# Layer norms that stand alone: squares in one full-width ScalarE step, summed by VectorE, and the turned rows copied by ScalarE

## The chip, the cores and the metric

The kernel runs on one core of a Trainium2 chip. The metric is the device time of one execution in microseconds (us). TensorE multiplies and transposes, VectorE and ScalarE do element-wise work, GpSimd a part of it, and SyncE issues most transfers.

## The reference

Four blocks run one after the other on 4 x 1024 tokens of width 128 in fp32. Each has a mixing part and a feed-forward part, and after each of the eight parts the sum with its input is normalised:

```
def _layernorm(x, axis=-1, eps=1e-05):
    m = jnp.mean(x, axis=axis, keepdims=True)
    v = jnp.var(x, axis=axis, keepdims=True)
    return (x - m) / jnp.sqrt(v + eps)
...
    x = _layernorm(x + _L0_attn_ref(x, ...), axis=-1)
    x = _layernorm(x + _L0_ffn_ref(x, ...), axis=-1)
...
    x = _layernorm(x + _L3_ffn_ref(x, ...), axis=-1)
```

The parts are a gated recurrence, a slot attention with a top-8 choice, a sparse attention on sampled keys, a two-way choice of experts, a linear attention, a top-2 mixture of experts, a state-space scan and a top-p mixture of experts.

## The kernel before

The activations lie transposed in the SBUF tensor `XT`, 128 channels on the partitions and 4096 tokens along the free dimension, in eight chunks of 512 (`NCH`, `ch`). `XK` is the same in token-major form, `ps` is PSUM in eight banks of 512 columns, `SM` holds small values and `TMP` working space. The kernel is one list of parts: stage 1, a fence, norm 1, a fence, stage 2 and so on. A `fence` makes TensorE, VectorE, ScalarE and GpSimd drain and wait for each other. Norms 6 and 7 are woven into other stages. Those after stages 1, 2, 3, 4, 5 and 8 are parts of their own (`LN_ALONE`), written by `layernorm(k)`. Norm 5 is "routed" (`LN_ROUTE`): it also makes router logits.

A norm's plan is a list of steps, and each engine walks through the same list and does its share of each step, in that order. For chunk i:

- `centre`: TensorE multiplies four 128x128 tiles by the centring matrix `cen`, which turns them to token-major form and subtracts the mean, into PSUM bank `pc[i % 4]`.
- `norm`: ScalarE squares the four tiles one after the other, each with an accumulator that gives the sum of squares (`ss`, line 206, and each is followed by an instruction that reads the accumulator), and then takes the root (`sd`, line 205). VectorE takes the reciprocal (`rs`, line 361) and multiplies the chunk into `XK` (line 210).
- `back`: TensorE transposes the chunk back (line 201) into one of three banks `pt`, and VectorE copies it to `XT` (line 209). In the routed norm ScalarE makes this copy (line 208).

The plan runs `centre` two chunks ahead of `norm`, and `back` one chunk behind. Semaphores of kind `Sig` tie the engines: `ln_cen`, `ln_sq`, `ln_sd`, `ln_rs`, `ln_xk`, `ln_tr`, `ln_xv` (rows copied by VectorE) and `ln_xa` (by ScalarE). In norm 2 TensorE also gathers sampled tokens, eight small matmuls after each turn. In norm 3 ScalarE also copies a piece of weights, 128x512, after each of the first six roots. Norm 8 is the last: it has no `back`, and SyncE stores each chunk of `XK` as the output.

Of the kernel before, what the change touches and what calls it, by code (L numbers as in the profile page):

```python
# [8 lines left out]
ALU = mybir.AluOpType  # L9
ACT = mybir.ActivationFunctionType  # L10
AX = mybir.AxisListType.X
# [6 lines left out]
NCH = T // CH  # L18
# [106 lines left out]
def g3(ap, n):  # L125
    return ap.rearrange("p (n k) -> p n k", n=n)
# [6 lines left out]
def ch(ap, i, k=CH):  # L133
    return ap[:, i * k:(i + 1) * k]


def tile(ap, i):
    return ap[:, i * 128:(i + 1) * 128]
# [12 lines left out]
def of(plan, step):  # L151
    return [a for s, a in plan if s == step]


def build(nc, wp, xT_d, sidx_d, cs_d, vecs_d, out_d):
# [3 lines left out]
    sem = Semaphores(lone)  # L159
# [21 lines left out]
    XT, XK, SM = mem["XT"][:, :], mem["XK"][:, :], mem["SM"][:, :]  # L181
# [3 lines left out]
    def w(name):  # L185
        r, o, c = at[name]
        return W[0:r, o:o + c]
# [5 lines left out]
    def mm(out, lhsT, rhs, start=True, stop=True, **k):  # L193
        return nc.tensor.matmul(out, lhsT, rhs, start=start, stop=stop, **k)  # L194
# [8 lines left out]
    def act(out, x, f, bias=0.0, scale=1.0, acc=None):  # L203
        if acc is None:
            return nc.scalar.activation(out, x, f, bias=bias, scale=scale)  # L205
        return nc.scalar.activation(out, x, f, bias=bias, scale=scale, accum_out=acc)  # L206

    acopy = lambda o, a: nc.scalar.copy(o, a)  # L208
    copy = lambda o, a: nc.vector.tensor_copy(o, a)  # L209
# [38 lines left out]
    LN_ROUTE = {5: ("rwT", 3)}  # L248
# [2 lines left out]
    ln_plans = {}  # L251
    for k in LN_ALONE:
        p = ln_plans[k] = [("centre", (k, 0)), ("centre", (k, 1))]
        for i in range(NCH):
            if i + 2 < NCH:
                p.append(("centre", (k, i + 2)))
            p.append(("norm", (k, i)))
            if k == 8:
                continue
            if i > 0:  # L260
                p.append(("back", (k, i - 1)))
            if k in LN_ROUTE and i > 1:
                p.append(("route", (k, i - 2)))
        if k < 8:
            p.append(("back", (k, 7)))
        if k in LN_ROUTE:
            p += [("route", (k, 6)), ("route", (k, 7))]
    ln_all = [x for k in LN_ALONE for x in ln_plans[k]]
    ln_cen = Sig(sem("ln_centred"), of(ln_all, "centre"))
    ln_sq = Sig(sem("ln_squares"), of(ln_all, "norm"))  # L270
    ln_sd = Sig(sem("ln_deviation"), of(ln_all, "norm"))
    ln_rs = Sig(sem("ln_reciprocal"), of(ln_all, "norm"))
    ln_xk = Sig(sem("ln_normed"), of(ln_all, "norm"))
    ln_tr = Sig(sem("ln_turned"), of(ln_all, "back"))
    ln_xv = Sig(sem("ln_rows_by_dve"), [(k, i) for k, i in of(ln_all, "back") if k not in LN_ROUTE])
    ln_xa = Sig(sem("ln_rows_by_act"), [(k, i) for k, i in of(ln_all, "back") if k in LN_ROUTE])
    ln_xh = Sig(sem("ln_high_parts"), [(k, i) for k, i in of(ln_all, "back") if k in LN_ROUTE])
    ln_xl = Sig(sem("ln_low_parts"), [(k, i) for k, i in of(ln_all, "back") if k in LN_ROUTE])
    ln_lg = Sig(sem("ln_logits"), of(ln_all, "route"))
# [11 lines left out]
    def layernorm(k):  # L291
        ar = arena()
        junk = [ar(512) for _ in range(2)]
        ss, rs, sd = SM[:, 0:32], SM[:, 32:64], SM[:, 480:512]
        src, plan = LN_SRC(k), ln_plans[k]
        last, routed = k == 8 or k == LAST, k in LN_ROUTE
        if last:
            plan = [(s, a) for s, a in plan if s in ("centre", "norm")]
        pc, pt = PS[0:4], PS[4:7]
        q4 = lambda ap, i: ap[:, 4 * i:4 * i + 4]  # L300

        def pe(e):
            for step, (_, i) in plan:
                if step == "centre":
                    if i >= 4:
                        e.wait_ge(*ln_xk.at((k, i - 4)))
                    for j in range(4):
                        r = mm(tile(pc[i % 4], j), tile(src, 4 * i + j), w("cen"))
                    r.then_inc(*ln_cen((k, i)))
                elif step == "back":  # L310
                    if i >= 3:
                        e.wait_ge(*(ln_xa if routed else ln_xv).at((k, i - 3)))
                    e.wait_ge(*ln_xk.at((k, i)))
                    for j in range(4):
                        r = turn(tile(pt[i % 3], j), tile(XK, 4 * i + j), w("ident"))
                    r.then_inc(*ln_tr((k, i)))
                    if k == 2:
                        e.wait_ge(*sa_sel.at("samples"))
                        b = i // 2
                        for c in range(4 * (i % 2), 4 * (i % 2) + 4):  # L320
                            r = mm(PS[7][:, b * 35:(b + 1) * 35], tile(XK, b * 8 + c), SO[:, c * 35:(c + 1) * 35], c == 0, c == 7)
                        if i == NCH - 1:
                            r.then_inc(*sa_xs("samples"))
                elif step == "route":
                    name, g = LN_ROUTE[k]
                    e.wait_ge(*ln_xa.at((k, i)))
                    e.wait_ge(s_w[g], 16)
                    for c in range(4 * i, 4 * i + 4):
                        r = mm(PS[7][:, c * 8:c * 8 + 8], tile(XT, c), w(name))
                    r.then_inc(*ln_lg((k, i)))  # L330

        def scalar(e):
            e.wait_ge(s_eps, 1)
            if k == 5:
                first_weights_high(e, 6)
            for step, (_, i) in plan:
                if step == "norm":
                    e.wait_ge(*ln_cen.at((k, i)))
                    for j in range(4):
                        c = 4 * i + j  # L340
                        r = act(tile(junk[i % 2], j), tile(pc[i % 4], j), ACT.Square, scale=128 ** -0.5, acc=ss[:, c:c + 1])
                    r.then_inc(*ln_sq((k, i)))
                    e.wait_ge(*ln_sq.at((k, i)))
                    act(q4(sd, i), q4(ss, i), ACT.Sqrt, bias=eps).then_inc(*ln_sd((k, i)))
                    if k == 3 and i < 6:
                        acopy(ch(top2_w[0], i), top2_src[i]).then_inc(*t2_high(i))
                elif step == "back" and routed:
                    e.wait_ge(*ln_tr.at((k, i)))
                    acopy(ch(XT, i), pt[i % 3]).then_inc(*ln_xa((k, i)))

        def dve(e):
            if k == 2:
                e.wait_ge(s_idx, 16)
                e.wait_ge(s_w[7], 16)
                copy(sif, sidx.bitcast(I32)).then_inc(*sa_num("samples"))
                e.wait_ge(*sa_num.at("samples"))
                tt(g3(SO, 8), sif.unsqueeze(1).to_broadcast([128, 8, 35]), spread(w("tokid"), 35), ALU.is_equal).then_inc(*sa_sel("samples"))
            for step, (_, i) in plan:
                if step == "norm":
                    e.wait_ge(*ln_sd.at((k, i)))  # L360
                    nc.vector.reciprocal(q4(rs, i), q4(sd, i)).then_inc(*ln_rs((k, i)))
                    e.wait_ge(*ln_rs.at((k, i)))
                    tt(g3(ch(XK, i), 4), g3(pc[i % 4], 4), spread(q4(rs, i), 128), ALU.mult).then_inc(*ln_xk((k, i)))
                elif step == "back" and routed:
                    x, h, l = ch(XT, i), ch(xh_all, i), ch(xl_all, i)
                    e.wait_ge(*ln_xa.at((k, i)))
                    copy(h, x).then_inc(*ln_xh((k, i)))
                    e.wait_ge(*ln_xh.at((k, i)))
                    minus(l, x, h).then_inc(*ln_xl((k, i)))
                elif step == "back":  # L370
                    e.wait_ge(*ln_tr.at((k, i)))
                    copy(ch(XT, i), pt[i % 3]).then_inc(*ln_xv((k, i)))

        def sync(e):
            if last:
                for i in range(NCH):
                    e.wait_ge(*ln_xk.at((k, i)))
                    nc.sync.dma_start(out_d.rearrange("b (n p) d -> p (b n) d", p=128)[:, 4 * i:4 * i + 4, :],
                                      g3(ch(XK, i), 4)).then_inc(s_out, 16)
        def pool(e):  # L380
            if k == 3:
                for i in range(6):
                    e.wait_ge(*t2_high.at(i))
                    gtt(ch(top2_w[1], i), top2_src[i], ch(top2_w[0], i).bitcast(F32), ALU.subtract).then_inc(*t2_low(i))
            if k == 5:
                first_weights_low(e, 6)
        return dict(pe=pe, dve=dve, act=scalar, pool=pool, sync=sync)


# [2342 lines left out]
    for k in range(1, LAST + 1):  # L2732
        s = stages[k - 1]()
# [156 lines left out]
```

## Time and profile before

| what | us |
|---|---|
| listed runs: lowest, median, highest of 3 | 2636.87, 2644.38, 2651.82 |
| profiled execution: span from first to last instruction | 2628.1 |
| TensorE busy (matmul) | 2322.3 (88%) |
| VectorE busy | 1851.4 (70%) |
| ScalarE busy | 1430.5 (54%) |
| GpSimd busy | 1004.3 (38%) |

The profiled execution is listed with its span only; its own time is none of the three. The three times count what lies before the first and after the last instruction too. The shares are means over the whole kernel, and say nothing of which engine holds up a given norm: for that the rows in order of time are read. The mean granted TensorE clock is 0.950 of its full speed.

### The profile page before, as it was taken

To read this page: it belongs to the slowest core of one execution; us is meant where nothing else is said; L and a number is where in the kernel's file an instruction comes from. 1 tells how busy PE (TensorE), PEld (TensorE's weight loads), DVE (VectorE), ACT (ScalarE), POOL (GpSimd) and SP (SyncE) were. 2 spreads that over 40 slices of the span, in tenths; PEclk is the share of its full clock that TensorE was granted. 3 is DMA by queue.
4 is the path that set the end of the run, shared out by engine and by line. 5 is a ranking of instruction groups with operands and counts; after the bars stand their busy time and mean duration, and the time that the engine had idled before them with its cause. 6 is when DMAs were issued, how large, how long until landed. Compare 5 with 4: busy or idle time off the path is not lost. (4 is left out here: it accounts for less than half of the span.)

```text
span 2628.1 us, 34742 instructions
## 1 busy us (share of the span) xinstructions
PE 2322.3 (88%) x12026; PEld 1723.2 (66%) x12026; DVE 1851.4 (70%) x3430; ACT 1430.5 (54%) x3023; POOL 1004.3 (38%) x791
## 2 busy tenths in 40 slices
PE   7686778898999999999989998688888886999998
PEld 3464556686899999899867777233333333677776
DVE  5667556676666666666577776488888886877776
ACT  6231232697544444444365554566666653877787
POOL 4000000210322222222125556589898985222222
PEclk8698899999999999999989999899999998999999
DMA  4000000000000000000011122223332330011112
GB/s 185 0 1 0 1 1 1 1 1 17 1 1 1 1 1 1 1 1 1 9 58 54 61 61 61 69 81 87 84 86 80 88 82 27 19 45 47 46 45 61
DMA packets 47551, 96.46 MB, mean 37 GB/s; under 512 B 5120, under 2 KB 9232, under 8 KB 46864
## 3 DMA queue, kind: packets, MB, share of 16 engines
q1 hardware_dynamic: 47344, 94.22, 11.9%
q8 instruction: 96, 1.57, 0.2%
q14 instruction: 79, 0.65, 0.1%
q0 software_dynamic: 32, 0.02, 0.1%
HBM read 91.34 MB, written 2.88 MB: 36 GB/s over the span
## 5 line engine op out<-in xcount | busy, mean ns | idle before, releaser
L194 PE MATMUL ps<-TMPr 128*128 128x512 f32 (+4 forms) x3840 | 956.4, 401 | 86.2 <-DVE TMP L210 26.5
L194 PEld LDWEIGHTS ps<-TMPr 128*128 128x128 f32 (+3 forms) x3840 | 718.2, 190 | 322.6 <-issue 77.6
L214 POOL TENSOR_TENSOR TMP<-TMP 128x512 f32<-128x512 f32 (+2 forms) x496 | 639.3, 1311 | 645.2 <-ACT TMP L205 463.4
L194 PE MATMUL ps<-TMP 128*128 128x65 f32 (+5 forms) x4352 | 514.2, 286 | 9.8 <-DVE TMP L213 7.8
L194 PEld LDWEIGHTS ps<-TMP 128*128 128x128 f32 (+3 forms) x4352 | 472.0, 191 | 62.5 <-issue 32.8
L205 ACT ACTIVATE TMP<-ps,W 128x256 f32<-128x256 f32 (+2 forms) x528 | 283.5, 584 | 303.2 <-DVE TMP L210 184.1
L194 PE MATMUL ps<-TMP,W 128*128 128x512 f32 (+5 forms) x720 | 367.8, 634 | 52.7 <-POOL TMP L214 14.7
L210 DVE TENSOR_TENSOR TMP<-ps,TMP 128x512 f32<-128x512 f32 (+1 forms) x434 | 252.5, 603 | 108.4 <-PE ps L194 48.8
L205 ACT ACTIVATE TMPr<-ps,W 128x512 fp32r<-128x512 f32 x352 | 242.9, 690 | 91.9 <-PE ps L194 72.1
L214 POOL TENSOR_TENSOR XT<-XT,XK 128x512 f32<-128x512 f32 x128 | 175.9, 1374 | 293.1 <-DVE XK L213 274.8
L194 PEld LDWEIGHTS ps<-TMP,W 128*128 128x128 f32 (+3 forms) x720 | 124.4, 191 | 220.4 <-issue 155.3
L213 DVE SCALAR_TENSOR_TENSOR TMPr<-ps,SM,XK 128x512 fp32r<-128x512 f32 x256 | 190.2, 750 | 91.5 <-ACT XK L205 89.3
L205 ACT ACTIVATE ps<-TMP,SM 128x512 f32<-128x512 f32 x256 | 175.0, 692 | 70.2 <-DVE TMP L2625 69.7
L208 ACT COPY TMP<-ps 128x260 f32<-128x260 f32 (+8 forms) x196 | 84.7, 438 | 221.9 <-PE ps L194 169.6
L194 PE MATMUL ps<-Wr 128*128 128x512 f32 (+1 forms) x768 | 190.3, 365 | 9.1 <-DVE Wr L210 9.0
L205 ACT ACTIVATE TMP<-ps 128x512 f32<-128x512 f32 x144 | 86.1, 598 | 139.4 <-PE ps L194 139.2
L2625 DVE TENSOR_TENSOR_SCAN TMP<-ps,SM,TMP 128x512 f32<-128x512 f32 x128 | 156.0, 1266 | 4.2 <-ACT ps L205 4.1
L2625 DVE TENSOR_TENSOR_SCAN TMP<-ps,TMP 128x512 f32<-128x512 f32 x128 | 148.9, 1206 | 12.7 <-ACT ps L205 8.3
L214 POOL TENSOR_TENSOR TMPr<-TMP,TMPr 128x512 fp32r<-128x512 f32 x72 | 93.8, 1304 | 133.8 <-ACT TMPr L208 133.8
L201 PE MATMUL ps<-W,TMP 128*128 128x128 f32 (+2 forms) x720 | 120.1, 282 | 22.3 <-DVE TMP L210 10.5
L205 ACT ACTIVATE XK<-TMPr,SM 128x512 f32<-128x512 f32 x192 | 137.3, 715 | 0.0
L194 PEld LDWEIGHTS ps<-Wr 128*128 128x128 f32 x768 | 120.9, 193 | 19.1 <-issue 9.4
(188 smaller groups left out, 2523.5 us busy)
## 6 DMA issues: line engine op xcount, KB each, us to landing
TMP<-rows SPq DMA_DIRECT2D x168, 256.0 KB, 3.5
TMP<-gates SPq DMA_DIRECT2D x112, 256.0 KB, 3.3
W<-wp SPq DMA_DIRECT2D x1, 4124.0 KB, 13.6
W<-wp SPq DMA_DIRECT2D x1, 3072.0 KB, 26.4
W<-wp SPq DMA_DIRECT2D x1, 2136.5 KB, 19.7
XT<-xT SPq DMA_DIRECT2D x4, 512.0 KB, 7.5
out<-XK SPq DMA_DIRECT2D x8, 256.0 KB, 2.3
W<-wp SPq DMA_DIRECT2D x1, 1993.0 KB, 15.4
```

What stands on the lines that cost most here:

```text
L194: return nc.tensor.matmul(out, lhsT, rhs, start=start, stop=stop, **k)
L201: turn = lambda out, x, ident: nc.tensor.transpose(out, x, ident)
L205: return nc.scalar.activation(out, x, f, bias=bias, scale=scale)
L208: acopy = lambda o, a: nc.scalar.copy(o, a)
L210: tt = lambda o, a, b, op: nc.vector.tensor_tensor(o, a, b, op)
L213: stt = lambda o, a, s, b, op0, op1: nc.vector.scalar_tensor_tensor(out=o, in0=a, scalar=s, in1=b, op0=op0, op1=op1)
L214: gtt = lambda o, a, b, op: nc.gpsimd.tensor_tensor(o, a, b, op)
L2625: nc.vector.tensor_tensor_scan(Hb[q % 4], Ab[q % 3], Ub[q % 6], first, ALU.mult, ALU.add).then_inc(*h_dve((a, x)))
```

## The change

For the norms that are not routed (1, 2, 3, 4 and 8) there is a new step `square`, one chunk ahead of `norm`. In it ScalarE squares the whole chunk in one instruction, 128x512, into `junk[i % 2]` in SBUF, without an accumulator, and VectorE sums each 128 columns of it with one `tensor_reduce` (line 372 of the changed kernel). ScalarE's square waits for the sum two chunks before, which frees `junk`, and the root waits for the sum of its chunk (`ln_sum`). The copy of the turned rows goes from VectorE to ScalarE. The routed norm is as before.

```diff
         p = ln_plans[k] = [("centre", (k, 0)), ("centre", (k, 1))]
+        p += [("square", (k, 0))] * (k not in LN_ROUTE)
         for i in range(NCH):
             if i + 2 < NCH:
                 p.append(("centre", (k, i + 2)))
+            if i + 1 < NCH and k not in LN_ROUTE:
+                p.append(("square", (k, i + 1)))
             p.append(("norm", (k, i)))
...
-    ln_sq = Sig(sem("ln_squares"), of(ln_all, "norm"))
+    ln_sq = Sig(sem("ln_squares"), [a for s, a in ln_all if s == "square" or s == "norm" and a[0] in LN_ROUTE])
+    ln_sum = Sig(sem("ln_sums"), of(ln_all, "square"))
...
-    ln_xv = Sig(sem("ln_rows_by_dve"), [(k, i) for k, i in of(ln_all, "back") if k not in LN_ROUTE])
-    ln_xa = Sig(sem("ln_rows_by_act"), [(k, i) for k, i in of(ln_all, "back") if k in LN_ROUTE])
+    ln_xa = Sig(sem("ln_rows_by_act"), of(ln_all, "back"))
...
-            plan = [(s, a) for s, a in plan if s in ("centre", "norm")]
+            plan = [(s, a) for s, a in plan if s in ("centre", "square", "norm")]
...
-                        e.wait_ge(*(ln_xa if routed else ln_xv).at((k, i - 3)))
+                        e.wait_ge(*ln_xa.at((k, i - 3)))
...
-                if step == "norm":
+                if step == "square":
                     e.wait_ge(*ln_cen.at((k, i)))
-                    for j in range(4):
-                        c = 4 * i + j
-                        r = act(tile(junk[i % 2], j), tile(pc[i % 4], j), ACT.Square, scale=128 ** -0.5, acc=ss[:, c:c + 1])
-                    r.then_inc(*ln_sq((k, i)))
-                    e.wait_ge(*ln_sq.at((k, i)))
+                    if i >= 2:
+                        e.wait_ge(*ln_sum.at((k, i - 2)))
+                    act(junk[i % 2], pc[i % 4], ACT.Square, scale=128 ** -0.5).then_inc(*ln_sq((k, i)))
+                elif step == "norm":
+                    if routed:
+                        e.wait_ge(*ln_cen.at((k, i)))
+                        for j in range(4):
+                            c = 4 * i + j
+                            r = act(tile(junk[i % 2], j), tile(pc[i % 4], j), ACT.Square, scale=128 ** -0.5, acc=ss[:, c:c + 1])
+                        r.then_inc(*ln_sq((k, i)))
+                        e.wait_ge(*ln_sq.at((k, i)))
+                    else:
+                        e.wait_ge(*ln_sum.at((k, i)))
                     act(q4(sd, i), q4(ss, i), ACT.Sqrt, bias=eps).then_inc(*ln_sd((k, i)))
...
-                elif step == "back" and routed:
+                elif step == "back":
                     e.wait_ge(*ln_tr.at((k, i)))
                     acopy(ch(XT, i), pt[i % 3]).then_inc(*ln_xa((k, i)))
...
-                if step == "norm":
+                if step == "square":
+                    e.wait_ge(*ln_sq.at((k, i)))
+                    nc.vector.tensor_reduce(q4(ss, i), g3(junk[i % 2], 4), AX, ALU.add).then_inc(*ln_sum((k, i)))
+                elif step == "norm":
                     e.wait_ge(*ln_sd.at((k, i)))
...
-                elif step == "back":
-                    e.wait_ge(*ln_tr.at((k, i)))
-                    copy(ch(XT, i), pt[i % 3]).then_inc(*ln_xv((k, i)))
```

What stands in ScalarE's row at the beginning of norm 1, before the change (`ln_centred` is `ln_cen`, `ln_squares` is `ln_sq`; the `SM<-SM` step is the root):

```order
L206 ACTIVATE TMP,SM<-ps 128x128 [waits ln_centred,s_eps,s_fence]
L206 ACTIVATE TMP,SM<-ps 128x128 x3
L205 ACT_TABLE_LOAD
L205 ACTIVATE SM<-SM 128x4 [waits ln_squares]
L206 ACTIVATE TMP,SM<-ps 128x128 [waits ln_centred]
L206 ACTIVATE TMP,SM<-ps 128x128 x3
L205 ACTIVATE SM<-SM 128x4 [waits ln_squares]
```

and with it (`ln_sums` is `ln_sum`, `ln_turned` is `ln_tr`):

```order
L205 ACTIVATE TMP<-ps 128x512 [waits ln_centred,s_eps,s_fence]
L205 ACTIVATE TMP<-ps 128x512 [waits ln_centred]
L205 ACT_TABLE_LOAD
L205 ACTIVATE SM<-SM 128x4 [waits ln_sums]
L205 ACTIVATE TMP<-ps 128x512 [waits ln_centred]
L205 ACTIVATE SM<-SM 128x4 [waits ln_sums]
L208 COPY XT<-ps 128x512 [waits ln_turned]
L205 ACTIVATE TMP<-ps 128x512 [waits ln_centred]
```

The squares of two chunks now stand ahead of the table load and the first root, and each copy of turned rows stands ahead of the square of the chunk three later.

VectorE's row at the same place, before the change (`ln_deviation` is `ln_sd`, `ln_reciprocal` is `ln_rs`):

```order
L361 RECIPROCAL SM<-SM 128x4 [waits ln_deviation,s_fence]
L210 TENSOR_TENSOR XK<-ps,SM 128x512 [waits ln_reciprocal]
L361 RECIPROCAL SM<-SM 128x4 [waits ln_deviation]
L210 TENSOR_TENSOR XK<-ps,SM 128x512 [waits ln_reciprocal]
L209 COPY XT<-ps 128x512 [waits ln_turned]
```

and with it:

```order
L372 TENSOR_REDUCE SM<-TMP 128x4 [waits ln_squares,s_fence]
L372 TENSOR_REDUCE SM<-TMP 128x4 [waits ln_squares]
L375 RECIPROCAL SM<-SM 128x4 [waits ln_deviation]
L210 TENSOR_TENSOR XK<-ps,SM 128x512 [waits ln_reciprocal]
L372 TENSOR_REDUCE SM<-TMP 128x4 [waits ln_squares]
L375 RECIPROCAL SM<-SM 128x4 [waits ln_deviation]
L210 TENSOR_TENSOR XK<-ps,SM 128x512 [waits ln_reciprocal]
```

The copies are gone from it, and a sum stands ahead of each reciprocal, that of the chunk after the reciprocal's own; two sums stand ahead of the first. TensorE's row is the same in both kernels.

## Rows read from the trace of the kernel before

**Rows 1.** The page: length of the profiled execution.

```profile
span 2628.1 us, 34742 instructions
```

**Rows 2.** Timeline of norm 4: start, length, engine, line, operation, [idle before].

```profile
633.89 0.28 ACT L206 ACTIVATE TMP<-ps 128x128 f32<-128x128 f32 x1 [4.03 <-PE ps L194]
...
637.58 0.68 DVE L209 COPY XT<-ps 128x512 f32<-128x512 f32 x1
...
637.79 0.30 ACT L205 ACTIVATE SM<-SM 128x4 f32<-128x4 f32 x1
637.82 0.60 PE L201 MATMUL ps<-W,XK 128*128 128x128 f32 x4
...
638.18 0.17 DVE L361 RECIPROCAL SM<-SM 128x4 f32<-128x4 f32 x1
...
638.38 0.69 DVE L210 TENSOR_TENSOR XK<-ps,SM 128x512 f32<-128x512 f32 x1
...
638.99 0.68 DVE L209 COPY XT<-ps 128x512 f32<-128x512 f32 x1
...
639.15 0.30 ACT L205 ACTIVATE SM<-SM 128x4 f32<-128x4 f32 x1
...
645.42 0.69 DVE L210 TENSOR_TENSOR XK<-ps,SM 128x512 f32<-128x512 f32 x1
...
646.26 1.04 PE L201 MATMUL ps<-W,XK 128*128 128x128 f32 x4 [0.78 <-DVE XK L210]
647.34 0.69 DVE L209 COPY XT<-ps 128x512 f32<-128x512 f32 x1 [0.63 <-PE ps L201]
```

**Rows 3.** Costs by shape: ScalarE and VectorE groups, mean ns of one.

```profile
L205 ACT ACTIVATE TMP<-ps,W 128x512 f32<-128x512 f32 x144 | 95.5, 688 | 115.2 <-PE ps L194 114.9
...
L205 ACT ACTIVATE TMP<-ps 128x512 f32<-128x512 f32 x144 | 86.1, 598 | 139.4 <-PE ps L194 139.2
...
L1196 DVE TENSOR_REDUCE SM<-ps 112x1 f32<-112x1024 f32 x20 | 24.5, 1225 | 20.0 <-PE ps L194 20.0
...
L713 DVE TENSOR_REDUCE TMP<-TMP 128x64 f32<-128x512 f32 x4 | 4.1, 1024 | 0.1
...
L685 DVE TENSOR_REDUCE TMP<-TMP 128x4 f32<-128x256 f32 x8 | 3.3, 412 | 6.9 <-POOL TMP L214 6.9
```

**Rows 4.** Timeline of norm 1: first squares, table load, first reciprocal, last copy.

```profile
53.84 0.28 ACT L206 ACTIVATE TMP<-ps 128x128 f32<-128x128 f32 x1 [7.26 <-PE ps L194]
...
55.00 1.28 ACT L205 ACT_TABLE_LOAD   x1
...
56.70 0.18 DVE L361 RECIPROCAL SM<-SM 128x4 f32<-128x4 f32 x1 [6.60 <-ACT SM L205]
...
68.15 0.69 DVE L209 COPY XT<-ps 128x512 f32<-128x512 f32 x1 [0.21 <-PE ps L201]
```

**Rows 5.** One stretch of norm 1: length, PE busy, weight loads, DVE, ACT, POOL, clock.

```profile
53.80:55.70 1.90, 1.90 (x11) 1.90 (x11) 0.00 (x0) 1.84 (x9) 0.00 (x0) 0.50 0.00 0
```

**Rows 6.** Timeline of norm 2: turns of chunks 4 and 5, last copy.

```profile
161.12 0.28 ACT L206 ACTIVATE TMP<-ps 128x128 f32<-128x128 f32 x1 [8.58 <-PE ps L194]
...
170.31 0.60 PE L201 MATMUL ps<-W,XK 128*128 128x128 f32 x4
...
172.54 0.60 PE L201 MATMUL ps<-W,XK 128*128 128x128 f32 x4
...
177.02 0.69 DVE L209 COPY XT<-ps 128x512 f32<-128x512 f32 x1 [0.34 <-PE ps L201]
```

**Rows 7.** Timeline of norm 3: first square, ScalarE's extra cast, last copy.

```profile
470.45 0.28 ACT L206 ACTIVATE TMP<-ps 128x128 f32<-128x128 f32 x1 [3.32 <-PE ps L194]
...
473.11 0.60 ACT L208 CAST TMPr<-W 128x512 fp32r<-128x512 f32 x1
473.30 0.18 DVE L361 RECIPROCAL SM<-SM 128x4 f32<-128x4 f32 x1 [4.21 <-ACT SM L205]
...
473.62 0.27 ACT L206 ACTIVATE TMP<-ps 128x128 f32<-128x128 f32 x1
...
488.08 0.69 DVE L209 COPY XT<-ps 128x512 f32<-128x512 f32 x1 [0.67 <-PE ps L201]
```

**Rows 8.** Timeline of norm 8: first square, first and last reciprocal.

```profile
2612.16 0.28 ACT L206 ACTIVATE TMP<-ps 128x128 f32<-128x128 f32 x1 [7.14 <-PE ps L194]
...
2615.01 0.18 DVE L361 RECIPROCAL SM<-SM 128x4 f32<-128x4 f32 x1 [5.57 <-ACT SM L205]
...
2624.46 0.18 DVE L361 RECIPROCAL SM<-SM 128x4 f32<-128x4 f32 x1 [0.46 <-ACT SM L205]
```


## The prediction

> **What bounds the kernel now.** Times are in us. I first looked for how much of the kernel the change can touch at all, then read the touched stretches row by row. The profiled execution spans 2628.1 [rows 1]; the listed runs have a median of 2644.4, 16.3 more, and that offset is kept in the sum. The change works only in five stretches, the norms alone after stages 1, 2, 3, 4 and 8. From first square to the end of the last step they last 15.0 [rows 4], 16.6 [rows 6], 18.3 [rows 7], 14.1 [rows 2] and 13.2 (the last reciprocal starts 12.3 after the first square, and the last multiply ends 0.9 after that, as at 638.18 to 638.38 + 0.69) [rows 2, 8]. Together that is 77.3, 2.9% of the span. Each is closed by fences, so nothing outside can overlap with it: what such a stretch loses or gains is lost or gained in full.
>
> Inside norm 4 the reader is to see VectorE without a gap: reciprocal at 638.18, multiply 0.20 later, copy of the turned rows 0.61 later, and a copy occupies it for 0.60 before the next reciprocal (637.58 to 638.18) [rows 2]. That is 1.41 a chunk. ScalarE repeats every 1.36 (637.79 to 639.15) [rows 2], hardly less. The two are balanced. Norm 1 runs the same program. Norm 8 has no turning, so it goes at ScalarE's pace: seven steps in 9.45, 1.35 each [rows 8]. Norm 2 goes at TensorE's pace, 2.23 a chunk (170.31 to 172.54) [rows 6], because the sample gathers lie between its turns. Norm 3 is ScalarE's, since it also makes weight parts there.
>
> **Prices.** The full-width Square has no row before. The same shape from PSUM without a bias tile takes 0.60, with one 0.69 [rows 3]; I take 0.60 and keep 0.69 as upper end. Its time until the next ScalarE step is 0.51, from the 512-wide cast that starts at 473.11 and is followed at 473.62 [rows 7]; the new ScalarE copy is priced the same way, 0.51 until the next and 0.59 until done. The sum over 512 elements into 4 has no row either. A contiguous reduction of 256 takes 0.41 and one of 1024 takes 1.225, which gives 0.68 for 512 on the line between them; a strided reduction of 512 takes 1.02 [rows 3]. Ours is contiguous, so I take 0.68 (0.60 until the next step), with 0.41 and 1.02 as ends. So on VectorE the added sum costs what the removed copy did, 0.60, and its work stays at 0.60 + 0.20 + 0.61 = 1.41. ScalarE's falls from 1.36 to 0.51 + 0.20 + 0.51 = 1.22.
>
> The interpolated 0.68 equals the 0.68 of the copy it replaces [rows 2, 3]. The Trainium skill (VectorE: DVE Perf Modes, Rules for kernel authors) calls `tensor_reduce` the slowest VectorE operation and advises restructuring, which speaks against adding 40 of them. Its perf-mode tier table gives a PSUM-source fp32 copy no fast mode, so by the page the exchange is even in norms with a copy and a pure loss in norm 8. The rows agree as far as they reach, and the sum would be the same by either.
>
> **Where the change adds a wait.** Equal work does not mean equal pace, since the order now closes a loop over two chunks. ScalarE's in-order list is: square i+1, root i, copy i-1, square i+2. The copy waits for the turn of i-1, and square i+2 is queued behind it although its data has long been there. Following it round: copy 0.51, square 0.60, hop to VectorE 0.10 (norm 1's load starts at 55.00 for 1.28, the root behind it takes 0.30, the reciprocal starts at 56.70 [rows 4]), sum i+2 0.60, reciprocal i+1 0.20, multiply 0.69, hop to TensorE 0.15 (645.42 + 0.69 to 646.26), turn 0.60 (637.82), hop 0.04 (646.26 + 1.04 to 647.34) [rows 2]. The total is 3.49 for two chunks, so 1.75 a chunk instead of 1.41. Chunks come in pairs: one step of 1.41, the next of 2.08. Before, VectorE's copy was last in its own list and nothing upstream was queued behind it on ScalarE.
>
> **Norm 4.** The head first. Before, the first reciprocal came 1.6 after the first square: in norm 1 the four squares with their reads end 1.16 after 53.84, where the load starts, and root and hop are 0.40 [rows 4]. Now square 0 and the wait of sum 0 are followed on VectorE by sum 1, whose square starts 0.9 after the first (a chunk's centring at the full clock is half of norm 1's 1.9, below): 0.9 + 0.60 + 0.10 + 0.60 = 2.2. Then 1.41 to reciprocal 1, two loops of 3.49 to reciprocal 5, 2.08 to reciprocal 6, 0.8 to reciprocal 7 (no sum is left ahead of it), and a tail of 0.20 + 0.69 + 0.15 + 1.04 + 0.04 + 0.59 = 2.7 with the slow last turn seen at 646.26 [rows 2]. Sum 16.2 against 14.1: **+2.0**.
>
> **Norm 1.** Same steps, but the centring runs at granted clock 0.50, the lower of TensorE's two levels (1.2 of 2.4 GHz): 11 matmuls in 1.90 [rows 5], and with two overlapping the edges a chunk of eight takes about 1.9. Square 1 therefore starts 1.9 after square 0, and the table load, which stood behind square 0 (55.00), now stands behind square 1: 55.7 + 0.6, load 1.3, root and hop 0.4, reciprocal at 58.0 instead of 56.70. From there 1.41 + 6.98 + 2.08 + 0.8 and a tail of 2.3 with a quick turn are 13.5, against 12.1 from 56.70 to the end of the last copy [rows 4]. **+2.7**.
>
> **Norm 2.** TensorE stays the bound, so the loop hides beneath 2.23 a chunk [rows 6]. What shows is the head's 0.6 and, once no centring is left and TensorE does a chunk in 1.3 (the last copy starts 0.64 after the last turn, so the three turns after 172.54 come in 3.84), one loop wait of 0.9 near the end. **+1.5**.
>
> **Norm 3.** Here ScalarE is the bound: before 1.36 + 0.51 for the cast = 1.87 a chunk, after 0.51 x 3 + 0.20 = 1.73, about the loop's 1.75. The head is 0.35 longer (square 1 before the load), six steps gain 0.13 each and the last one, where the cast is gone, 0.6. **-1.0**.
>
> **Norm 8.** Head 0.35 longer, then VectorE's 1.41 against 1.35; but the last sum comes ahead of reciprocal 6, so the last step is only 0.8. That is 0.8 + 6 x 1.41 = 9.3 against 9.45 [rows 8]. **+0.2**. Its output transfers start with the multiplies and move by the same.
>
> Sum: 2.0 + 2.7 + 1.5 - 1.0 + 0.2 = +5.4, so 2633.5 of span and, with the offset, 2644.4 + 5.4 = **2649.8**, 0.2% more. The other edits (fewer instructions to fetch, the lost accumulator reads) cost nothing: ScalarE is never the bound after them except in norm 3, where they are counted.
>
> **Rivals.**
> - The loop does not show, because the copy is ready earlier than I reckon or ScalarE runs on: then VectorE's 1.41 rules. Norms 1, 4 and 2 keep only their heads, +1.3, +0.6 and +0.6, the others as above: +1.7, 2646.1. For it: ScalarE has 0.2 to spare a chunk. Against it: the order, which nothing relaxes. Chance 0.16.
> - The sum costs what the strided one does, 1.02. VectorE needs 1.75 a chunk even without the loop, the loop 3.83; norm 8 is hit in full. That adds 0.34 to every second chunk of norms 1 to 4, some 12, and to seven of norm 8: +6.4, 2656.2. With the squares and copies at 0.69 too, 2659. At 0.41 instead it takes off 2.4. Chance 0.12 for dear, 0.06 for cheap.
> - Slower by far: the clock. TensorE gets more pauses at 1.75 a chunk, and may be granted the lower level. Centring and turn then take 1.9 + 1.04 = 2.9 [rows 2, 5], so norms 1 and 4 lose 1.2 on seven chunks each, and norm 2, if it is caught, up to 2.2 on eight: 34 over my sum, 2684. It decides from 7.8 more than I reckon, that is, norm 2 caught for four chunks. For it: the last turns of norm 4 already take 1.04 instead of 0.60 [rows 2]. Against it: TensorE pauses in norm 3 much longer per chunk (1.87 pace), and norm 2 leaves it no pauses. Chance 0.03.
> - A gain that can be measured would have to be 13 of the 77.3, a sixth of all five norms. No price above leads there unless the sum were nearly free. Chance 0.02.
>
> **How the numbers follow.** A measurement of this kernel tells about 0.5% from no change; that is 13.2. My forecast has 0.61. It, the hidden loop, and the cheap and the dear sum all lie within 0.5%; only the clock lies beyond. Runs of the same kernel spread over 15, so a true +5 can be read a little beyond: I move 0.05 from same to slower and 0.02 to faster. Same 0.88, slower 0.08, faster 0.04. The cost bounds give 2646 to 2659; the runs' spread, 7.5 either side for one and about half for a median, widens this to 2638 to 2662.
>
> **What would show it.** Squares of 128x512 at 0.60, eight a norm, without accumulator reads; reductions at 0.68 on VectorE. Reciprocals in norm 4 in pairs, 1.41 and about 2.08 apart, and squares that wait for TensorE only because a copy stands ahead. Table load of norm 1 at about 56.3. Norm 3 shorter by one. Wrong: even steps of 1.41 (the loop does not bind), a reduction of 1.0, a granted clock of 0.5 in the middle of norms 1, 2 or 4, or any difference outside the five stretches.

## The result, and the profile after

| | us |
|---|---|
| kernel before, median of 20 runs (lowest, highest) | 2644.43 (2636.81, 2653.74) |
| changed kernel, median of 20 runs | 2654.88 (2642.42, 2670.25) |
| ratio, 95% interval | 1.0035 (1.0019 to 1.0052) |

The change costs about 0.35%, and the interval of the ratio lies above 1. The forecast was 2649.8.

The page of the changed kernel gives this span, 13.7 longer than that of [rows 1]:

```profile
span 2641.8 us, 34502 instructions
```

First norm 4 of the changed kernel in order of time, to be laid beside [rows 2]. Columns as there.

```profile
638.55 3.84 PE L194 MATMUL ps<-W,XT 128*128 128x128 f32 x32 [0.89 <-DVEq L230]
...
642.68 0.67 DVE L372 TENSOR_REDUCE SM<-TMP 128x4 f32<-128x512 f32 x1
...
643.27 0.17 DVE L375 RECIPROCAL SM<-SM 128x4 f32<-128x4 f32 x1
...
643.51 0.58 ACT L208 COPY XT<-ps 128x512 f32<-128x512 f32 x1 [1.20 <-PE ps L201]
644.00 0.60 ACT L205 ACTIVATE TMP<-ps 128x512 f32<-128x512 f32 x1
...
644.48 0.30 ACT L205 ACTIVATE SM<-SM 128x4 f32<-128x4 f32 x1
...
644.63 0.69 DVE L372 TENSOR_REDUCE SM<-TMP 128x4 f32<-128x512 f32 x1 [0.47 <-ACT TMP L205]
...
645.24 0.17 DVE L375 RECIPROCAL SM<-SM 128x4 f32<-128x4 f32 x1
...
645.44 0.69 DVE L210 TENSOR_TENSOR XK<-ps,SM 128x512 f32<-128x512 f32 x1
...
646.18 0.42 PEld L201 LDWEIGHTS ps<-W,XK 128*128 128x128 f32 x4 [0.60 <-DVE XK L210]
646.18 0.66 PE L201 MATMUL ps<-W,XK 128*128 128x128 f32 x4 [0.41 <-DVE XK L210]
...
646.64 0.17 DVE L375 RECIPROCAL SM<-SM 128x4 f32<-128x4 f32 x1
...
646.88 0.58 ACT L208 COPY XT<-ps 128x512 f32<-128x512 f32 x1 [0.70 <-PE ps L201]
```

The reader is to see two things. The square at 644.00 starts 0.49 after the copy at 643.51, and that copy had waited 1.20 for its turn. The square's own data had been there since 642.39 at the latest, when the centring of the first four chunks ended (638.55 + 3.84). And the reciprocal at 645.24 comes 1.97 after the one at 643.27, the next at 646.64 only 1.40 later. The reciprocals of the whole norm are 1.40, 1.97, 1.40, 1.96, 1.46, 1.97 and 0.81 apart, where before it was 1.29 once and then 1.40 to 1.42.

Who waited for whom in norm 4 (us in total, times, longest):

```profile
ACT XT L208 <- PE ps L201: 4.9, 7, 1.5
...
PE ps L201 <- DVE XK L210: 3.5, 5, 1.3
```

ScalarE's copy waits for TensorE's turn seven times in the norm's eight chunks, and everything behind it on ScalarE waits with it. That wait did not exist before, when VectorE copied.

The prices, from the groups by shape (busy us, mean ns of one), first ScalarE's, then VectorE's:

```profile
L205 ACT ACTIVATE TMP<-ps 128x512 f32<-128x512 f32 x184 | 109.9, 598 | 174.6 <-PE ps L194 174.3
...
L208 ACT COPY XT<-ps 128x512 f32<-128x512 f32 x56 | 32.6, 583 | 29.7 <-PE ps L201 29.4
```

```profile
L372 DVE TENSOR_REDUCE SM<-TMP 128x4 f32<-128x512 f32 x40 | 27.3, 683 | 23.0 <-ACT TMP L205 22.6
```

The square has joined the group of 598 ns (184 instead of 144), the copy takes 583 ns, and the sum 683 ns.

The head of norm 1 in order of time, beside [rows 4]:

```profile
54.06 0.60 ACT L205 ACTIVATE TMP<-ps 128x512 f32<-128x512 f32 x1 [7.26 <-PE ps L194]
...
55.68 0.60 ACT L205 ACTIVATE TMP<-ps 128x512 f32<-128x512 f32 x1 [1.03 <-PE ps L194]
56.30 1.28 ACT L205 ACT_TABLE_LOAD   x1
...
57.92 0.18 DVE L375 RECIPROCAL SM<-SM 128x4 f32<-128x4 f32 x1 [0.92 <-ACT SM L205]
```

The second square waits until 55.68 for a centring at the lower clock, the table load stands behind it at 56.30 instead of 55.00, and the first reciprocal follows at 57.92, 3.86 after the first square instead of 2.86.

Measured in this way, from first square to the end of the last copy or multiply, the five norms compare as follows.

| norm | before | forecast | changed kernel |
|---|---|---|---|
| 1 | 15.0 | +2.7 | 17.6 (+2.6) |
| 2 | 16.6 | +1.5 | 17.9 (+1.3) |
| 3 | 18.3 | -1.0 | 17.6 (-0.7) |
| 4 | 14.1 | +2.0 | 15.8 (+1.6) |
| 8 | 13.2 | +0.2 | 13.2 (0.0) |
| together | 77.3 | +5.4 | 82.1 (+4.8) |

So 4.8 of the 13.7 lie in the norms. The rest lies where the change touches nothing, which the prediction had named as a sign of being wrong. The largest piece is stage 5: 665.2 from norm 4 to norm 5 before, 670.3 now, and 1.5 in norm 5 itself. Two windows that begin at the same matmul, near the end of stage 5, show it, the first of the kernel before, the second of the changed kernel (from:to, length, then busy time and instructions of TensorE, weight loads, VectorE, ScalarE and GpSimd, granted clock, transfers):

```profile
1288.59:1302.59 14.00, 13.44 (x118) 12.72 (x117) 5.95 (x15) 2.30 (x5) 0.00 (x0) 1.00 0.00 1
```

```profile
1296.00:1310.00 14.00, 13.44 (x76) 12.19 (x76) 4.55 (x9) 1.92 (x4) 0.00 (x0) 0.63 0.00 1
```

Before, TensorE had the full clock (2.4 GHz) in the whole window; in this execution of the changed kernel it had 0.63 on average, so part of it at the lower level of 1.2 GHz, and 14 us hold 76 matmuls instead of 118.

### The profile page after: what moved, and what is told of

It is laid out like the page before. It is cut to its first block and busy times, and to the rows that moved or that the text cites. A ratio compares the mean times of both kernels' runs of the same rounds, so it can differ in the third digit from the quotient of the medians.

```text
span 2641.8 us, 34502 instructions
## 1 busy us (share of the span) xinstructions
PE 2332.6 (88%) x12026; PEld 1734.7 (66%) x12026; DVE 1857.3 (70%) x3438; ACT 1424.3 (54%) x2775; POOL 1004.4 (38%) x791
## 3 DMA queue, kind: packets, MB, share of 16 engines
q1 hardware_dynamic: 47344, 94.22, 11.9%
## 5 line engine op out<-in xcount | busy, mean ns | idle before, releaser
L205 ACT ACTIVATE TMP<-ps 128x512 f32<-128x512 f32 x184 | 109.9, 598 | 174.6 <-PE ps L194 174.3
## 6 DMA issues: line engine op xcount, KB each, us to landing
W<-wp SPq DMA_DIRECT2D x1, 1993.0 KB, 15.3
```

## The experiments

Each ran in rounds with the kernel before on the same chip. The table has all of them; "clock" is the mean over a kernel's runs of the granted TensorE clock, and "norms" the sum of the five norms in its profile. The first row takes together the 88 runs of the kernel before whose clock is listed; the 20 beside the first measurement have none.

| kernel | median, us | before in the same job | ratio (95%) | clock | norms, us |
|---|---|---|---|---|---|
| before | 2643.4 (88 runs) | | | 0.9439 | 77.3 |
| changed | 2654.88 | 2644.43 | 1.0035 (1.0019 to 1.0052) | 0.9407 | 82.1 |
| changed, again | 2650.84 | 2643.36 | 1.0026 (1.0006 to 1.0045) | 0.9422 | 82.6 |
| pure delay of 4.9 | 2651.85 | 2642.61 | 1.0027 (1.0006 to 1.0049) | 0.9417 | 76.8 + 4.9 |
| the same, TensorE busy | 2651.92 | 2643.36 | 1.0035 (1.0013 to 1.0056) | 0.9438 | 78.0 + 4.9 |
| loop opened | 2642.98 | 2642.61 | 1.0001 (0.9977 to 1.0025) | 0.9445 | 75.6 |
| squares only | 2661.79 | 2642.61 | 1.0064 (1.0044 to 1.0084) | 0.9401 | 88.6 |
| copies only | 2663.49 | 2642.61 | 1.0074 (1.0048 to 1.0099) | 0.9387 | 88.5 |
| changed, TensorE busy | 2652.54 | 2643.36 | 1.0026 (1.0002 to 1.0050) | 0.9447 | 81.9 |
| mixed | 2635.43 | 2643.36 | 0.9988 (0.9962 to 1.0015) | 0.9439 | 71.8 |
| mixed, again | 2633.12 | 2644.71 | 0.9975 (0.9953 to 0.9997) | 0.9453 | 72.5 |
| loop opened, early load | 2645.49 | 2644.71 | 1.0010 (0.9988 to 1.0033) | 0.9423 | 74.0 |

**The loop opened.** One list is reordered:

```diff
-        p += [("square", (k, 0))] * (k not in LN_ROUTE)
+        p += [("square", (k, 0)), ("square", (k, 1))] * (k not in LN_ROUTE)
...
-            if i + 1 < NCH and k not in LN_ROUTE:
-                p.append(("square", (k, i + 1)))
             p.append(("norm", (k, i)))
+            if i + 2 < NCH and k not in LN_ROUTE:
+                p.append(("square", (k, i + 2)))
```

> The changed kernel with the square of chunk i+2 put behind the root of chunk i and ahead of the copy of chunk i-1, on ScalarE and in VectorE's list. Loop theory: the copy no longer stands ahead of the square, the ring over two chunks falls to about 2.6 us, and VectorE's own 1.41 us rules: even steps of 1.41 in norms 1 and 4 instead of 1.40 and 1.96 in turn. Norm 1 16.1, norm 2 17.2, norm 3 17.1, norm 4 14.7, norm 8 13.2 us, 3 us less than the changed kernel together. Price theory (the uneven steps come from the costs of sum and square, not from the order): steps and norms as in the changed kernel.

Norm 4 of it in order of time:

```profile
643.66 0.17 DVE L375 RECIPROCAL SM<-SM 128x4 f32<-128x4 f32 x1
...
643.90 0.58 ACT L208 COPY XT<-ps 128x512 f32<-128x512 f32 x1 [0.49 <-PE ps L201]
644.38 0.30 ACT L205 ACTIVATE SM<-SM 128x4 f32<-128x4 f32 x1
...
644.79 0.60 ACT L205 ACTIVATE TMP<-ps 128x512 f32<-128x512 f32 x1
...
645.06 0.17 DVE L375 RECIPROCAL SM<-SM 128x4 f32<-128x4 f32 x1
```

Behind the copy there now stands the root, for which 0.3 suffices, and the reciprocals come at 643.66 and 645.06, 1.40 apart, as they do in the whole norm but for its last step (1.12). The same instructions with the same prices, in another order, so the uneven steps came from the order. The norms last 15.7, 17.0, 15.8, 13.9 and 13.2, together 75.6 instead of 82.1, and the kernel is level with before. Norm 3 gained more than expected (15.8 instead of 17.1); 0.8 of it is its head, which had the full clock here and the lower one in the changed kernel's profile. The last turns of norms 1 and 4 were on the full clock here too, 0.4 quicker each. Without these three about 4.8 of the 6.5 are left for the order.

**One part alone.** First the squares and sums, with VectorE's copy kept:

```diff
-                elif step == "back":
+                elif step == "back" and routed:
                     e.wait_ge(*ln_tr.at((k, i)))
                     acopy(ch(XT, i), pt[i % 3]).then_inc(*ln_xa((k, i)))
...
+                elif step == "back":
+                    e.wait_ge(*ln_tr.at((k, i)))
+                    copy(ch(XT, i), pt[i % 3]).then_inc(*ln_xv((k, i)))
```

> One part of the change alone: full-width squares summed by VectorE, but VectorE keeps the copy of the turned rows. VectorE then needs 0.60 + 0.20 + 0.61 + 0.60 = 2.0 us a chunk and is the bound in norms 1, 3 and 4: norm 1 20.4, norm 2 18, norm 3 19.5, norm 4 18.3, norm 8 13.2 us, about 12 us over the kernel before in the norms together, ratio about 1.005. If the sum were hidden or much cheaper than its 0.60, the steps would stay below 2.0.

```profile
662.40 0.17 DVE L376 RECIPROCAL SM<-SM 128x4 f32<-128x4 f32 x1
...
662.60 0.69 DVE L210 TENSOR_TENSOR XK<-ps,SM 128x512 f32<-128x512 f32 x1
...
663.21 0.68 DVE L209 COPY XT<-ps 128x512 f32<-128x512 f32 x1
...
663.81 0.68 DVE L373 TENSOR_REDUCE SM<-TMP 128x4 f32<-128x512 f32 x1
...
664.40 0.17 DVE L376 RECIPROCAL SM<-SM 128x4 f32<-128x4 f32 x1
```

That is norm 4, VectorE alone: reciprocal, multiply, copy, sum, reciprocal without a gap, 2.00 for the round. The norms last 19.5, 18.4, 19.8, 17.7 and 13.2, 11.3 over before.

Then the copies alone, with four squares and their accumulators as before:

```diff
-                elif step == "back" and routed:
+                elif step == "back":
                     e.wait_ge(*ln_tr.at((k, i)))
                     acopy(ch(XT, i), pt[i % 3]).then_inc(*ln_xa((k, i)))
...
-                elif step == "back":
-                    e.wait_ge(*ln_tr.at((k, i)))
-                    copy(ch(XT, i), pt[i % 3]).then_inc(*ln_xv((k, i)))
```

> The other part alone: four squares with accumulators as before, and ScalarE copies the turned rows. ScalarE then needs 1.36 + 0.50 = 1.86 us a chunk, in norm 3 2.37: norm 1 17.6, norm 2 17.5, norm 3 21.3, norm 4 16.7, norm 8 13.2 us, about 9 us over the kernel before in the norms together, ratio about 1.0035. If the copy fitted into ScalarE's waits, the steps would stay near 1.41.

```profile
655.74 0.30 ACT L205 ACTIVATE SM<-SM 128x4 f32<-128x4 f32 x1
655.94 0.57 ACT L208 COPY XT<-ps 128x512 f32<-128x512 f32 x1
656.07 0.18 DVE L360 RECIPROCAL SM<-SM 128x4 f32<-128x4 f32 x1 [0.95 <-ACT SM L205]
...
656.41 0.28 ACT L206 ACTIVATE TMP<-ps 128x128 f32<-128x128 f32 x1
...
657.59 0.30 ACT L205 ACTIVATE SM<-SM 128x4 f32<-128x4 f32 x1
```

ScalarE's roots of norm 4 are 1.85 apart (655.74 and 657.59), and it has no gap. The norms last 18.7, 18.2, 21.1, 17.2 and 13.2, 11.2 over before; the first copy costs one long step (2.55 in norm 1, 2.36 in norm 4) that I had left out. Each part alone makes one engine the bound. Together they balance, and then the order decides.

**Where the rest comes from.** The kernel before with idle additions at the ends of three norms:

```diff
+            if k in (1, 2, 4):
+                e.wait_ge(*ln_xk.at((k, 7)))
+                for q in range(4 if k == 1 else 2):
+                    tt(idle[q], ch(XK, q), ch(XK, q), ALU.add)
```

> The kernel before, with four, two and two idle VectorE additions at the ends of norms 1, 2 and 4, 0.61 us each: 4.9 us of pure delay, as much as the changed kernel loses in its five norms (4.8 us in its profile), and nothing else changed. Theory A (the rest of the changed kernel's loss comes from TensorE's clock, whose steps fall elsewhere on the same work once the work is shifted): the time rises by clearly more than the delay, by about 10 us, and the profile shows dips of the granted clock at other places than before. Theory B (the rest has to do with how the changed norms use the engines): the time rises by the delay alone, 4.9 us, ratio 1.0019.

Its median rose by 9.2, near theory A, but the interval of the ratio (1.0006 to 1.0049) holds the pure 1.0019 too. Alone it decides nothing. The changed kernel once more:

> The changed kernel once more. Its twenty runs had a mean granted clock of 0.9407, the thirty of before 0.9438, and at equal clock it was 4.1 us longer by a line through all runs (2.2 us for each 0.001 of clock); its median was 10.4 us longer. If the lower clock belongs to the change: again about 0.941 and about 9 us. If it was chance: a clock near 0.944 and a median about 5 us over before. In the profile the five norms again last 4.8 us longer together in either case.

The median is 7.5 over before, the clock 0.9422: between the two cases. Its profile shows that the surplus wanders. Stage 5, which was 5 longer in the first profile, has its old 665.0 again. Instead it is stage 2 (from the end of norm 1 to norm 2's first square) that takes 102.5 instead of 92.3. The windows of that stage, the kernel before first, then this run:

```profile
68.84:161.12 92.28, 62.29 (x275) 44.07 (x276) 52.92 (x190) 21.85 (x42) 5.74 (x8) 0.72 0.00 0
```

```profile
70.08:172.53 102.45, 73.09 (x274) 48.22 (x275) 52.91 (x189) 22.07 (x43) 5.74 (x8) 0.62 0.00 0
```

The work is the same, and the clock 0.62 instead of 0.72. The end of the stage had the lower level throughout, and still had it at the head of norm 2, which begins at 172.53 and lasts 0.8 longer than in the first profile:

```profile
144.00:175.00 31.00, 26.99 (x73) 15.31 (x72) 10.09 (x17) 6.19 (x17) 0.00 (x0) 0.50 0.00 0
```

The delay was then run with TensorE kept at work in it:

```diff
+            if k in (1, 2, 4):
+                for q in range(12 if k == 1 else 6):
+                    mm(tile(pc[0], q % 4), tile(XK, q % 4), w("cen"))
```

> The kernel with the pure delay of 4.9 us at the ends of norms 1, 2 and 4 (it had a mean clock of 0.9417 and 9 us), with TensorE now given filler matmuls during the delay: 12, 6 and 6, of 0.22 us each, into a PSUM bank that is free by then. Pause theory (a norm during which TensorE stands still more often leaves the lower clock to what comes next): the mean clock returns to before's 0.944, the time is 4 to 5 us over before. Chance theory: the clock has nothing to do with such pauses; it lies anywhere between 0.941 and 0.945.

The timeline of its TensorE at the end of norm 1 shows the fillers, 24 records in 2.84 behind the last turn, and that the next stage starts 0.54 after them:

```profile
68.33 0.63 PE L201 MATMUL ps<-W,XK 128*128 128x128 f32 x4 [0.78 <-DVE XK L210]
68.80 2.84 PE L194 MATMUL ps<-W,XK 128*128 128x128 f32 x24
72.18 0.38 PE L194 MATMUL ps<-W 64*128 64x1 f32 x2 [0.54 <-DVEq L230]
```

The mean clock did return to 0.9438. The median did not follow: 8.6 over before, nearly as without the fillers (9.2), though the interval (1.0013 to 1.0056) also holds the 1.0019 of the delay alone. The profiles show where the clock was gained and where it was lost. Two windows of the delay without fillers, then two of the delay with them, behind norm 1 and at the end of stage 2:

```profile
70.00:76.00 6.00, 3.79 (x8) 1.69 (x9) 2.85 (x11) 0.92 (x1) 0.00 (x0) 0.50 0.00 0
144.50:164.20 19.70, 15.69 (x61) 9.26 (x60) 9.21 (x15) 4.71 (x14) 0.00 (x0) 0.83 0.00 0
```

```profile
70.00:76.00 6.00, 4.92 (x25) 2.60 (x23) 3.17 (x12) 1.79 (x2) 0.00 (x0) 1.00 0.00 0
144.50:172.60 28.10, 24.10 (x58) 12.41 (x57) 9.20 (x15) 4.81 (x14) 0.00 (x0) 0.50 0.00 1
```

With the fillers the full clock held behind norm 1, and the end of stage 2 was at the lower level instead. The stage took 103.0, and 94.9 without them. Whether the fillers caused the second is open; the repeated changed kernel, without fillers, had it too. The changed kernel with fillers:

```diff
+                    if k in (1, 3, 4):
+                        for q in range(1 if i < 7 else 4):
+                            mm(tile(PS[7], q), tile(XK, 4 * i + q), w("cen"))
```

> The changed kernel, with one filler matmul of 0.22 us on TensorE after each turn of norms 1, 3 and 4, and four after the last turn, into the PSUM bank that is unused there. TensorE then works 1.55 of 1.68 us a chunk instead of 1.33. Pause theory: the mean clock rises from 0.9407 to about 0.944, and the time falls from about 10 over before to about 5. Chance theory: the clock stays as the repeated changed kernel shows it in the same job. The norms' own lengths stay within 0.5 us of the changed kernel's.

The same again: clock 0.9447, the highest but one, and a median 9.2 over before, with the norms at 81.9; this interval (1.0002 to 1.0050) too holds the 5 us that the pause theory expected. So the medians speak against the pause theory, and do not exclude it. A line through all runs (below) says more: at equal clock the two kernels with fillers are 8.4 and 10.1 over before, and the same kernels without them 3.4, and 4.6 and 3.8. A mean granted clock over the whole span is no measure of what the clock costs when filler work raises it.

**A version from both.** The form of before in norms 1, 2, 4 and 8, the loop-free new form in norm 3, and one early root:

```diff
+            if k in (1, 3, 8):
+                act(sd[:, 31:32], eps, ACT.Sqrt)
```

> The kernel before in norms 1, 2, 4 and 8, the loop-free order of the new form (root of chunk i, square i+2, copy i-1) in norm 3 alone, and in norms 1, 3 and 8 a one-column root at the very start, so that the table load of 1.28 us lies in the wait for the first centring. Expected: norm 1 14.2, norm 2 16.6, norm 3 14.9, norm 4 14.1, norm 8 11.9 us, together 5.5 us less than before, ratio about 0.998. If the load isn't hidden by the wait: norm 1 and norm 8 as before, and only norm 3 shorter by 2.5.

The head of norm 8 in order of time:

```profile
2607.27 0.20 ACT L205 ACTIVATE SM<-SM 128x1 f32<-128x1 f32 x1 [4.49 <-POOLq L238]
...
2607.30 3.39 PE L194 MATMUL ps<-W,XT 128*128 128x128 f32 x28 [2.25 <-POOLq L238]
2608.49 0.28 ACT L206 ACTIVATE TMP<-ps 128x128 f32<-128x128 f32 x1 [1.01 <-PE ps L194]
...
2609.67 0.30 ACT L205 ACTIVATE SM<-SM 128x4 f32<-128x4 f32 x1
...
2610.07 0.18 DVE L380 RECIPROCAL SM<-SM 128x4 f32<-128x4 f32 x1 [4.23 <-ACT SM L205]
```

The one-column root at 2607.27 is over before the first centring is, with the load ahead of it, and from the first square to the first reciprocal it is 1.58 instead of the 2.85 of [rows 8]. The norms last 13.9, 16.6, 15.3, 14.1 and 11.9, together 71.8, 5.4 less than before, as expected. The ratio did not yet exclude 1. Repeated:

> The mixed kernel once more, to narrow its interval: 0.9988 with bounds on both sides of 1 so far, 5.4 us shorter in its norms and 4.1 us shorter at equal clock. Expected again 0.998 to 0.999, and norms within 0.1 us of 13.9, 16.6, 15.3, 14.1 and 11.9 where the clock is the same.

0.9975 (0.9953 to 0.9997), and norms of 14.8, 16.6, 15.3, 13.9 and 11.9. Norm 1 is 0.9 longer than the first time; its first two steps took 1.64 and 1.70 instead of 1.44 and 1.42. Both medians (2635.4 and 2633.1) are below those of both kernels. The early root with the new form everywhere:

> The new form in all five norms in the loop-free order, with the table load moved into the wait for the first centring in norms 1, 3 and 8. The load was worth 1.3 us in norm 8 of the mixed kernel and about 1.1 in norm 1. Expected: norm 1 14.6, norm 2 17.0, norm 3 15.3, norm 4 13.9, norm 8 11.9 us, together 72.7, 4.5 us less than before, and nearly what the mixed kernel reaches. If full-width squares gained something beside norm 3, it would be below the mixed kernel's 71.8.

The norms last 14.6, 17.0, 15.1, 13.9 and 13.4, together 74.0; norm 8 kept the lower clock at its head, so its first reciprocal was 2.9 after the first square (29 centring matmuls took 6.28, in the mixed kernel 28 took 3.39). Even at the 11.9 expected it would be 72.5, no better than the mixed kernel. Beside the first profile of the mixed kernel norms 1 and 2 are longer (14.6 and 17.0 against 13.9 and 16.6), and norm 4 is level (13.9 and 14.1). The new form pays in norm 3 alone, where ScalarE was the bound: 15.3 instead of 18.3 in the mixed kernel, of which the early load, 1.28 long, can be at most 1.3 (an estimate). The median, level with before, doesn't show the 3.3 saved in the norms.

## Why the prediction was right, and where it was off

**What bounds the norms.** Right. VectorE's 1.41 and ScalarE's 1.36 were balanced, and both parts of the change alone moved the bound as priced: 2.00 and 1.85 a chunk.

**Prices.** Right, nearly to the digit: square 598 ns, copy 583, sum 683, against 0.60, 0.59 and 0.68. The dear and the cheap sum fall.

**The loop.** Right in place and kind, shown by the reordered kernel. Its length was 3.49 in the sum and is 3.37 (copy at 643.51 to copy at 646.88). Two hops were too dear. For the one to TensorE 0.15 was read at the end of norm 4, while in the loop the turn starts 0.05 after the multiply (645.44 + 0.69 to 646.18); the one to VectorE is 0.03 instead of 0.10 (644.00 + 0.60 to 644.63). The turn was too cheap, 0.66 instead of 0.60.

**Norm by norm.** The total, +4.8 for +5.4, is closer than its parts. The heads of norms 4 and 1 were too long in the sum: the first reciprocal comes 2.07 and 3.86 after the first square (2.2 and 4.2 reckoned), and the steps behind it are together 0.3 shorter in each. In norm 1 a slow last turn gave that back: the tail is 2.8 for 2.3. In norm 3 the head was mis-sized, 1.0 longer instead of 0.35, because its centring had the lower clock in this profile (0.50 from 477.1 to 479.1); with the full clock, as in the opened loop's profile, it is 0.2 longer. Its steps gained 1.6 where 1.4 was reckoned. Norm 8 came out at 0.0 for 0.2. That these errors nearly cancel is luck.

**The offset.** Wrong. I took the 16.3 between the profiled span and the median as time outside the span, and kept it. The runs since list span and time together, and the two differ by 1.8 (2641.8 and 2643.55 for the changed kernel's profile). The profile of before is simply of a quick execution, about 2630 by that measure, when the 88 runs go from 2627 to 2655. The sum added a difference to the median, so the forecast didn't suffer. But it tells how to read the two spans. The profile of the changed kernel is of a quick execution as well: 2643.6, 11.3 below its median, when that of before is 14.5 below its own. So 3 of the difference of 13.7 come from that, 4.8 from the norms, and about 6 are the same surplus that the medians have.

**The size.** The forecast of +5.4 fits the norms; the median moved by 10.4 and, repeated, by 7.5. The norms' profiles account for 4.8 and 5.4 of that, and 2 to 6 are unaccounted for; the intervals, 5.0 to 13.8 and 1.6 to 11.9 over before, leave open how much of that is noise. The prediction had nothing outside the norms, so its time lies 5.1 below the measured one: the mechanism in the norms was right, and whatever is real of the surplus beside them was put at nothing. A line through the runs of all kernels, with one slope and a level for each kernel, gives 2.1 less for each 0.001 of clock; at equal clock the changed kernel is 4.6 and 3.8 over before, with an error of 0.6 each. That this is near the norms' own 4.8 proves little: the same line puts the kernel with the opened loop 2.6 over before, whose norms are 1.7 shorter, and the delay of 4.9 at 3.4. The surplus does go together with a lower clock: 0.9413 over its 32 runs against 0.9439. Where the clock is lost differs from profile to profile (stage 5 in one, stage 2 in the other). The rival that named the clock put it inside norms 1, 2 and 4; in the first profile these have 0.89, 1.00 and 0.93, and before 0.93, 1.00 and 0.94, so hardly any of it is there. Whether slower norms make such a loss in later stages likelier stays open. For it speaks that the kernels with longer norms or a delay, and no fillers, all lie between 0.9387 and 0.9422 and the kernel before at 0.9439; against it, that the kernel with the opened loop and the early load, with short norms, lies at 0.9423 as well. Twelve runs of a kernel don't settle that.

## What to carry to other kernels

Balanced totals per engine are not enough: when a step is moved to another engine, follow its result once round that engine's in-order list, and look at what now stands behind a step that waits. Here the order of two lines was worth 6.5 of 82 us in the profiles, and about 4.8 without what the clock gave to the better one: as much as the whole change had cost. A full-width step with a separate reduction pays where ScalarE is the bound and VectorE is free, not where both are level. And a single profile must be placed among the runs before its span is compared with another's.

## What the runs showed of the hardware

- A stage without any change in it, stage 2, took 92 to 93 us in seven of the twelve profiles (the delay of 2.4 apart) and 98 to 103 in the other five. The two whose windows are shown had granted clocks of 0.72 and 0.62. That alone moves the kernel by 0.4%, as much as the whole change.
- Filler matmuls lift the granted clock (0.9417 to 0.9438, and 0.9413 to 0.9447), and the kernel was no quicker: 2651.9 with and without them for the delay, and for the changed kernel 2652.5 with them, 2650.8 and 2654.9 without.
- A contiguous `tensor_reduce` of 512 fp32 elements to 4 takes 683 ns, the strided one of [rows 3] 1024. The Trainium skill (VectorE: DVE Perf Modes, Rules for kernel authors) calls the operation the slowest of VectorE; here it took the same as the 684 ns copy from PSUM that it replaced, and the scans of the same width on VectorE (`tensor_tensor_scan`, 128x512) took 1206 and 1266 ns, so this trace doesn't bear that out for fp32.
